# A recurrent layer with mixture of experts on one core: the slot lists move into the first 34 groups of the scan, the barrier ahead of the scan goes, and the norm's polynomial is evaluated by Horner's form

## The reference, cut to what matters

```python
def step(h, inp):                       # h: 4 x 256 x 16
    h = dAt * h + dBt * xt[..., None]
    h_norm = sqrt(sum(h * h, axis=(1, 2)))          # one number per batch
    h = h * minimum(20.0 / (h_norm + 1e-08), 1.0)
    y = einsum('bdn,bn->bd', h, Ct) + Dp * xt
    ...
s = scan(step) over the 1024 steps
# 8 experts, top 2 of them per token, each takes at most 1280 token slots
logits = xt @ w_g ;  top 2 ;  rank of a token within its expert by a running count
h = gelu(exp_batches @ c_fc) ;  exp_out = h @ c_proj ;  out = weights @ exp_out
x = x + s * silu(out)
```

## Time and profile before

| | before |
|---|---|
| median of 3 runs | 1744.08 us (1744.07, 1744.08, 1752.08) |
| the profiled execution: its time | 1751.14 us |
| its span | 1749.4 us |
| scan, first L779 to last | 124.8 to 1723.4 us |
| DVE busy | 93% of the span |
| PE, ACT, POOL busy | 75%, 70%, 47% |
| granted TensorE clock | 0.875 of full |

### The profile page before, as it was taken

The page is one execution under the profiler, slowest core; times in us unless marked ns, Lnnn a source line. Parts: engine busy times, 40 slices in busy tenths (PEclk is TensorE's granted clock), DMA queues, the critical chain, the costliest instruction groups (busy, mean ns, idle before and its releaser), DMA issues.

```text
span 1749.4 us, 36383 instructions
## 1 busy us (share of the span) xinstructions
PE 1318.9 (75%) x9480; PEld 1158.5 (66%) x9480; DVE 1629.2 (93%) x11602; ACT 1232.3 (70%) x3156; POOL 814.2 (47%) x1295
## 2 busy tenths in 40 slices
PE   6589796987868688877869689776959777765663
PEld 5478685876757577766758578665858666654552
DVE  8559999999989999999999999999999989999978
ACT  4528886868677677868778677957768595867452
POOL 4034544545445445454554554454555445444432
PEclk9569898998989899898989889888989988886886
DMA  9811001100101020101101110111001100002245
GB/s 317 277 60 37 19 26 61 40 20 25 61 22 34 19 68 28 32 22 45 45 19 34 43 50 19 35 43 43 25 16 49 43 22 20 13 19 88 68 151 197
DMA packets 77488, 98.77 MB, mean 56 GB/s; under 512 B 7776, under 2 KB 66272, under 8 KB 77280
## 3 DMA queue, kind: packets, MB, share of 16 engines
q1 hardware_dynamic: 68096, 75.25, 13.2%
q0 software_dynamic: 7680, 20.98, 3.7%
q10 hardware_dynamic: 1504, 0.22, 0.1%
HBM read 56.71 MB, written 39.71 MB: 55 GB/s over the span
## 4 chain that ended last, share of the span: by engine, by line
DVE 61%; POOL 18%; PE 10%; issue 6%; ACT 3%; DMA 1%; POOLq 0%; SPq 0%; DVEq 0%; ACTq 0%
DVE arena L811 13%; DVE arena L785 10%; DVE arena L779 9%; POOL arena L555 8%; DVE arena L793 8%; DVE arena L800 8%; DVE arena L815 6%; POOL moe L535 5%; POOL xrow L530 4%; DVE arena L782 3%; DVE arena L797 3%; PE ps L1212 2%; PE ps L1150 2%; PE ps L1235 2%; PE ps L1231 1%
## 5 line engine op out<-in xcount | busy, mean ns | idle before, releaser
L555 POOL TENSOR_TENSOR arena<-arena,neghalf 128x1 f32<-128x1 f32 x1025 | 591.7, 577 | 791.1 <-DVE arena L782 782.8
L811 DVE SCALAR_TENSOR_TENSOR arena<-arena 128x128 f32<-128x128 f32 x1024 | 363.3, 355 | 38.1 <-POOL arena L555 32.4
L1231 PE MATMUL ps<-ident,arena 128*128 128x128 f32 x1024 | 215.8, 338 | 229.2 <-ACT arena L923 160.6
L1231 PEld LDWEIGHTS ps<-ident,arena 128*128 128x128 f32 x1024 | 180.6, 243 | 270.7 <-ACT arena L923 165.5
L1247 PE MATMUL ps<-arena,wf 128*128 128x256 f32 x1280 | 308.4, 390 | 9.0 <-issue 9.0
L1235 PE MATMUL ps<-arena,pick 128*128 128x128 f32 x2048 | 301.3, 295 | 14.7 <-ACT arena L1020 14.7
L1020 ACT ACTIVATE arena<-ps,arena 128x128 f32<-128x128 f32 x1024 | 292.1, 376 | 28.3 <-PE ps L1235 27.7
L793 DVE CUSTOM_DVE_ANT_0 arena<-arena 128x128 f32<-128x128 f32 x1024 | 293.1, 286 | 10.9 <-ACT arena L1020 5.8
L785 DVE CUSTOM_DVE_ANT_0 arena<-arena 128x128 f32<-128x128 f32 x1024 | 299.1, 292 | 0.0
L1263 PE MATMUL ps<-wp,arena 128*128 128x256 f32 x1280 | 298.5, 387 | 0.2 <-ACT arena L1028 0.2
L779 DVE TENSOR_TENSOR arena<-arena 128x128 f32<-128x128 f32 x1024 | 293.3, 286 | 5.4 <-ACT arena L1020 5.4
(11 more groups left out here) (160 smaller groups left out, 1608.9 us busy)
## 6 DMA issues: line engine op xcount, KB each, us to landing
arena<-in_x SPq DMA_DIRECT2D x16, 512.0 KB, 9.3
moe<-zeros SPq DMA_DIRECT2D x8, 1024.0 KB, 10.5
wf<-in_c_fc SPq DMA_DIRECT2D x8, 1024.0 KB, 5.2
wp<-in_c_proj SPq DMA_DIRECT2D x8, 1024.0 KB, 5.5
arena<-dx SPq DMA_DIRECT2D x66, 64.0 KB, 2.0
ys<-arena SPq DMA_DIRECT2D x66, 64.0 KB
xnd<-arena SPq DMA_DIRECT2D x8, 512.0 KB, 5.4
dx<-arena SPq DMA_DIRECT2D x8, 512.0 KB, 5.5
```

The costliest lines, as they stand in the source:

```text
L555: g.tensor_tensor(sv[:, slot, 1:2], mx, neghalf[:, 0:1], ALU.pow).then_inc(s_ready, 1)
L811: v.scalar_tensor_tensor(hr[:, slot, :], vv, sv[:, before, 1:2], ur[:, slot, :], ALU.mult, ALU.add)\
L1231: last = t.transpose(ps[q % 2][:, j * P:(j + 1) * P], tanhb[:, f, :, s], ident[:, :])
```

## The change

**1. Step.** The reciprocal is dropped. `q = (sums_vv * s + sums_uv) * s + e` is evaluated by one scan instruction over two elements, which needs `s` alone. The scale 1/CLAMP^2 moves into the two sums. `terms` (4 columns per step: the sum of vv, that of uv, e, B) takes the place of `sums` and `ring_be`.

**2. Slot lists.** They leave the stage ahead of the scan. ACT builds the one-hots as relu(1 - |col - value|), 4 pairs per two groups (`distances` in odd groups, `hits` in even ones), PE's `slots` follows one pair of groups later, up to group 33; DVE closes the lists at step 140 (`slot_lists`), and POOL's first two gathers follow steps 141 and 142. The barrier `loop_go` goes; POOL clears `hr` after `route_ready`.

**3. Expert work** is spread over groups 39 to 232 in place of 1 to 231, by the same rule. The tables of `at_step` and of the three preparation tables shift with it. `logs_of(2)` moves from ahead of the scan into group 1.

**4. Decays.** The four exponentials at the end of a period become one of 2048 columns (`decay_op`) in the last group of the period and one in the third group of each of the next three blocks. The tanh tiles go into 15 groups instead of 16.

**5. Preparation.** ACT's and DVE's order of the first chunks changes: logs and `add_logs` two chunks earlier, `scan_input` inside the chunk loop, the tanh tiles in four lots of 8, and the exponential for the routing weights after one decay instead of ahead of four.

```diff
-            decay_ops(0).then_inc(decay_ready, 1)
-            act.sem_inc(loop_go, 1)
-            act.wait_ge(loop_go, 5)
+            act.wait_ge(lg_ps, 1)
+            act.wait_ge(xT_out, 16 * (CH - 1))
...
+            def distances(g):
...
+                for c in range(4):
+                    k, j = divmod(4 * g + c, JT)
+                    a.activation(lohot[:, g % 2, c, :], cols, ACT.Abs, bias=lo[:, k, j:j + 1])
+                    last = a.activation(hihot[:, g % 2, c, :], cols[:, 0:SC], ACT.Abs, bias=hi[:, k, j:j + 1])
+                last.then_inc(apart, 1)
+
+            def hits(g):
+
+                act.wait_ge(apart, g + 1)
+                part = lohot[:, g % 2].rearrange("p n c -> p (n c)")
+                a.activation(part, part, ACT.Relu, scale=-1.0, bias=1.0)
+                for c in range(4):
+                    k, j = divmod(4 * g + c, JT)
+                    last = a.activation(hihot[:, g % 2, c, :], hihot[:, g % 2, c, :], ACT.Relu, scale=rowid[:, k, j:j + 1],
+                                        bias=rowneg[:, k, j:j + 1])
+                last.then_inc(hot_ready, 1)
...
-                        last = tanh_ops(1 - f, 2 * (QPB * (blk % 4) + q), 2)
+                        first = 32 * (quad % 16) // 15
+                        last = tanh_ops(1 - f, first, 32 * (quad % 16 + 1) // 15 - first)
+                        if quad % 16 == 14:
+                            last.then_inc(tanh_done, 1)
+                    elif blk + 4 < NBLK:
+                        act.wait_ge(tanh_done, blk // 4 + 2)
+                        decay_op(1 - f, 0)
+                    if q == 2 and blk % 4 < 3:
+                        decay_op(f, blk % 4 + 1)
...
+                    if quad % 2 == 1 and quad // 2 < TILES // 2:
+                        distances(quad // 2)
+                    if quad % 2 == 0 and 1 <= quad // 2 <= TILES // 2:
+                        hits(quad // 2 - 1)
                 if blk % 4 == 3 and blk + 4 < NBLK:
-                    last.then_inc(tanh_done, 1)
-                    act.wait_ge(tanh_done, blk // 4 + 2)
-                    decay_ops(1 - f).then_inc(decay_ready, 1)
```

```diff
-        QUADS, MOE_QUADS, COMBINE_AT = NT // QUAD, 232, 240
+        QUADS, MOE_AT, MOE_QUADS, COMBINE_AT = NT // QUAD, 39, 233, 240
...
-            by_quad[1 + (n + w[3] // 2) * (MOE_QUADS - 1) // total].append(w)
+            by_quad[MOE_AT + (n + w[3] // 2) * (MOE_QUADS - MOE_AT) // total].append(w)
...
-                    dve.wait_ge(m_ready, now)
-                    v.reciprocal(sv[:, before, 0:1], mx)
...
-                    v.tensor_tensor_reduce(out=junkq, in0=sums, in1=sv[:, before, :], scale=1.0 / CLAMP ** 2, scalar=ring_be[:, slot, 1:2],
-                                           op0=ALU.mult, op1=ALU.add, accum_out=qv).then_inc(q_ready, 1)
+                    v.tensor_tensor_scan(horner, sv[:, before, 1:2].broadcast_to([P, 2]), terms[:, slot, 1:3], terms[:, slot, 0:1],
+                                         ALU.mult, ALU.add).then_inc(q_ready, 1)
...
+            pool.wait_ge(route_ready, 1)
+            g.memset(hr, 0.0).then_inc(h_ready, 1)
```

More of the change, by code:

```diff
@@ L119, in build @@
         junk = take(2 * P).rearrange("p (f d) -> p f d", f=2)
-        junkq = take(2)
+        horner = take(2)
+        qv = horner[:, 1:2]
         ac = take(2)
-        sums = take(2)
-        qv = take(1)
         mx = take(1)
@@ L567, in _ @@
                     kind, i, c = at_step[step]
-                    if kind == "turn" and c == 0:
+                    if kind == "first" and c == 0:
+                        pool.wait_ge(xn_out, 16 * CH)
+                        pool.wait_ge(padz, 16 * (NB + 1))
+                        pool.wait_ge(slots_ready, 1)
+                    elif kind == "turn" and c == 0:
                         pool.wait_ge(xt_tp, i + 1)
@@ L585, in _ @@
                     kind, i, c = at_step[step]
-                    if kind == "turn":
+                    if kind == "first":
+                        gather(c, slot_src[:, c:c + 1])
+                    elif kind == "turn":
                         gather(c, slot_src[:, 2 * (i + 1) + c:2 * (i + 1) + c + 1])
@@ L664, in _ @@
                     v.tensor_scalar(a16c[:, :], alog, -DT_C / 16.0, None, ALU.mult).then_inc(a_ready, 1)
-                if i in (4, 5):
+                if i in (2, 3):
                     for c in range(4):
-                        add_logs(i - 4, c)
+                        add_logs(i - 2, c)
+                if i in (5, 6):
+                    for c in range(4):
+                        scan_input(i - 5, c)
             dve.wait_ge(consts, CONSTS)
-            for h in range(2):
-                for c in range(4):
-                    scan_input(h, c)
             hops = [0]
@@ L697, in _ @@
             v.tensor_copy(ohb, ohf).then_inc(rt_in, 1)
+            for h in range(2):
+                norm_of_input(h)
             dve.wait_ge(gap_exp, 1)
@@ L742, in _ @@
-            for h in range(2):
-                norm_of_input(h)
-            for i in range(CH):
-                one_hot(i)
-            dve.wait_ge(route_ready, 1)
-            dve.sem_inc(loop_go, 1)
-            dve.wait_ge(hot_used, CH)
-            hop(v.tensor_scalar(acc, ps[7][:, 0:SC], float(2 * TOK), None, ALU.add))
-            hop(v.tensor_scalar(free, acc, float(2 * TOK), pcol, ALU.is_equal, ALU.mult))
-            hop(v.tensor_tensor(acc, acc, free, ALU.add))
-            v.tensor_copy(slot_dst[:, :], acc)
@@ L784, in _ @@
                     dve.wait_ge(v_ready, now)
-                    v.tensor_tensor_reduce(out=junk[:, 0, :], in0=vv, in1=ur[:, slot, :], scale=2.0, scalar=0.0,
+                    v.tensor_tensor_reduce(out=junk[:, 0, :], in0=vv, in1=ur[:, slot, :], scale=2.0 / CLAMP ** 2, scalar=0.0,
                                            op0=ALU.mult, op1=ALU.add, accum_out=ac[:, 1:2])
@@ L808, in _ @@
                         norm_of_input(norm_at[step][0])
+                    if step == SLOTS_AT:
+                        slot_lists()
                     dve.wait_ge(s_ready, now)
@@ L1002, in _ @@
                     act.wait_ge(norm_ready, blk // 4 + 1)
-                a.activation(ring_be[:, half * BLK:(half + 1) * BLK, :], be[:, span(blk * BLK, BLK), :],
+                a.activation(terms[:, half * BLK:(half + 1) * BLK, 2:4], be[:, span(blk * BLK, BLK), :],
                              ACT.Copy).then_inc(be_stage, 1)
@@ L1049, in _ @@
                         inputs_out_of_psum(blk + 1)
-                    if blk + 4 < NBLK:
+                    if blk + 4 < NBLK and quad % 16 < 15:
                         if blk % 4 == 0 and q == 0:
@@ L1225, in _ @@
                     if q == 1:
-                        output(blk, blk * BLK + 1, blk % 2)
+                        output(blk, max(1, blk) * BLK + 1, blk % 2)
                     pe.wait_ge(da_done, quad + 1)
```

201 lines of the change are left out of this document (93 added, 108 removed).

## The result

The changed kernel takes 1799.46 us (median of 4 runs, 1798.66 to 1801.48) against 1744.07 of the kernel before on the same chip; the ratio is 1.0309, 95% interval 1.0286 to 1.0332. It is slower by 3.1%, and 20 us beyond the range that the prediction gave. The profiled execution took 1798.66 us, its span is 1796.9.

What follows compares the result with a forecast made beforehand. The serial scan on DVE and POOL was taken to set the time; 1749.4 - 41 - 19 + 31 + 6 - 18 + 34 - 2 was given as 1740 us. Range 1702 to 1780 us, leaving out 2 in 10.

Steps and rivals of the forecast that it cites:

- The start: Ahead of the scan: earlier routing and moved slot lists let it run as if begun at 83.4, not 124.8: -41 us.
- The step: Each of 864 scan steps without a DMA gains 0.022 us from the two-element scan instruction: -19 us.
- The ring: One scan step's dependency loop through DVE and POOL's 0.54 us, 1.48 us around; the reciprocal lies outside it.
- rival (d): In the scan step, the scan instruction doesn't overlap, 0.045 us lost per step: +58, 1780 us; chance 0.09.
- The shortage in the first 34 groups: Early scan: ACT's one-hots and other work make DVE wait, 22 us of it at step 35: +31 us.
- The old waits for logarithms: DVE's two waits for logs behind four exponentials, 15.0 us together, go, with 2.5 at step 8: -18 us.
- The rest of the experts' phase: After the early groups, denser tiles and yrow_free cap ACT's lead, making seven places late: +34 us.
- Rival (c): ACT with PE bounds the whole experts' phase, at 101 us costing 3 in each of 12 periods: 1776; chance 0.20.
- Rival (a): Whole kernel as forecast, 1725 to 1755 us, with yrow_free capping ACT's lead in the experts' phase; chance 0.40.
- (f): On ACT, a table switch costs 2.66 us, adding 12 x 8 over the periods: 1836 us; chance 0.04.
- The signs: DVE idle 15 to 28 us at step 35, over 5 at 499 and 611; their absence would refute the prediction.
- The end: Combining stage: three exponentials with loads move in, the old block of exponentials ahead goes: -2 us.

Runs made afterwards that it cites:

- Horner's form alone: The kernel before with only the reciprocal dropped and the step's polynomial evaluated by the two-element scan instruction: 1740.2 us, 0.9956.
- the early copy: The changed kernel with ACT's copy of the next block's inputs moved ahead of the last group's gelu, PE's transpose earlier too: 1765.1 us, 1.0082.
- the kernel with all four edits: The changed kernel with inputs copied out earlier, a second yrow buffer, add_logs and scan_input places 8 steps later, zeros stored later: 1699.7 us, 0.9703.
- the dense kernel: The kernel before with only the experts' 40 tiles moved into groups 39 to 232, exponentials still together: 1797.9 us, 1.0284.

## Why the prediction was wrong, step by step

**The start** (-41): -33.5 as measured by 91.3 for 124.8. The end of the routing came 4 us later than counted, and the load of dx wasn't counted at all: it took 8.6 us here, behind the stores, and not its usual 1.9. The prediction noted PE's first output, but not what it waits for besides `hr`.

**The step** (-19): -9. The ring and the missing share of the reciprocal were right. The scan instruction was taken to last 0.16 with a pace of 0.08; it lasts 0.22, and its pace is 0.13, over the 0.12 from which I had called rival (d) the case. It still isn't (d): it loses nothing to the old operation's 0.14. DVE's operations do overlap: L775 starts 0.27 after L771, which takes 0.35, so the DRAIN rule of the Trainium skill (VectorE: DVE Perf Modes, Terms) doesn't describe these starts. Leaving out the reciprocal gave back 0.010 us per step, not its 0.156.

**The shortage in the first 34 groups** (+31): right in size. Steps 7, 11, 15, 35, 51, 99 and 115 are 34.0 us too long together, and leaving the one-hots out gives 33.5. It is spread otherwise: 13.7 at step 35 for 22, and 5.4 and 5.7 at 51 and 115 for 2.5.

**The old waits for logarithms** (-18): the mechanism holds alone (-13). In the denser kernel it is undone: at step 499 DVE waits 12.9 us for them, more than before. That the runs of 1744.07 and 1752.08 differ by one such wait isn't shown, and one profile speaks against it: with Horner's form alone, at 1733.5 us, both waits are there (7.6 and 8.0), and what is missing are the long steps 992 to 1019, 10.7 us in the profile of before.

**The rest of the experts' phase** (+34) is the step that failed. Taking the DMAs' shift (+12), the step (-6), the old waits (-15) and the small things (+3.5) from the 62.1 leaves 68 us, twice the term; the version without these waits is 71 faster in this stretch. Two things were wrong. First, late places were counted by the work between a release of `yrow` and the place, "with about 1 us of PE's waits each", as if ACT had its full lead again before each. Second, the sum of 99 us against 98 was worked out, and then I wrote "I count nothing for it". This was the answer. The kernels with one limit taken away show it. With the second `yrow` buffer alone, ACT never waits for `yrow_free`, and from step 163 to 928 a period still takes 103.6 us where DVE needs 99.2 (18.4 of it ACT's waits for PE): this is what ACT and PE need together, 4.6 more than my sum. The terms behind it, by the changed kernel from 300 to 1500 us: ACT stands 194 us for PE (ten rows, from 40.7 down to 4.7) and 42.5 for `yrow_free`, in 11.4 periods of 105.1, which is 17 and 3.7 per period. So the waits for PE were nearly right at 18, and ACT's own part is 84.4 and not 81.

A feeder that needs more than the consumer never regains a lead, so nearly every place comes late, and what is lost at one isn't won back at the next. Rival (c) names this mechanism, at 3 us per period where the second buffer leaves 4.4. Rival (a)'s cap is real too: with the early copy alone the chain through PE is shorter (from step 163 to 928 ACT waits 9.6 us per period for PE), but it waits 9.3 for `yrow_free`, and the period is 103.4. So over the 99.2 of the kernel with all four edits either limit alone costs about 4 us per period and both 6. They hold at once and overlap; the prediction set (a) and (c) against each other.

The signs couldn't tell them apart. What would have called the prediction wrong didn't come: DVE waits 13.4 us at step 35 (15 to 28 forecast), 12.9 and 13.4 at steps 499 and 611. Of the sign of (c) half is there: from 300 to 1500 us ACT waits no more for DVE (29.9 before), but still for POOL, and DVE's idle time ahead of L754 is only 20.5 us in the whole run, 6.1 of it at the start.

Against (c) the prediction set "PE no longer stands still for 10 us at each period's end". True, it is 3.6 now, but the spread exponentials made waits of about 5 us at the other boundaries, as in the rows at 1108 to 1113, and these the prediction didn't look for: it asked what the loads cost ACT, not what stands behind them on ACT that PE waits for.

**The table switch** (f): the load is 1.28 and the next operation starts 1.29 after it (1106.57, 1107.86), as in the earlier trace rows, against the 2.66 for a switch in the Trainium skill (ScalarE: Activation LUTs, What ACT_TABLE_LOAD costs). In the kernel with all four edits the number of loads costs nothing (1699.7 us with the spread, 1702.8 without). In the changed kernel, where ACT and PE bind, putting the exponentials together took 14 us from steps 163 to 928, with the loads, the order at the boundary and the late logarithms mixed; there it stays open.

**The end** (-2): right.

**The sum.** The terms as written add up to 1742, not 1740, which changes nothing in the account.

What stays open: how much of the 34 us of the early copy is owed to the table loads; the two kernels that speak to it differ in more. And why the dense kernel with the exponentials together loses as much as the changed one is shown only for the 40 us that the second buffer and the 17 that the early copy win back there.

## What to carry to other kernels

When two engines that feed a serial consumer need, with their waits for each other, as much time per period as the consumer does, count every us beyond that once per period. Then look for what each of them waits for on the other's queue at a block's boundary: the place of a 0.27 us copy, last in its group, was worth 34 us. A cap on the lead (a single buffer) and a lack of throughput hide each other; test them together before either is dropped. And a load moved to the start of a stage must be counted with the transfers that were issued ahead of it.

## What was not expected of the hardware

The two-element scan instruction takes 0.22 us and its successor starts 0.13 after it, barely less than the multiply with its read-out (0.14). A load of 64 KB that lands in 1.9 us in the median took 8.6 behind some MB of stores issued ahead of it on the same queue. An exponential of 2048 columns takes 1.91 us and a table load 1.28, the mean of 99 (groups of ACT, with mean ns behind the busy time):

```profile
L884 ACT ACTIVATE arena<-arena 128x2048 f32<-128x2048 f32 x64 | 122.5, 1914 | 0.6
L884 ACT ACT_TABLE_LOAD x51 | 65.4, 1283 | 0.5
L1013 ACT ACT_TABLE_LOAD x48 | 61.6, 1283 | 24.6 <-PE ps L1236 23.9
```
